# Moving the turns of the row maxima four jobs later in the attention of a transformer block

## The reference, cut to what matters

```python
q = rmsnorm(apply_rope(q, cos, sin), qn_w)
k = rmsnorm(apply_rope(k, cos, sin), kn_w)
k = jnp.repeat(k, rep, axis=2)
v = jnp.repeat(v, rep, axis=2)
scores = jnp.einsum('bthd,bshd->bhts', q, k) / np.sqrt(HD)
scores = jnp.where(causal[None, None], scores, -jnp.inf)
attn = jax.nn.softmax(scores, axis=-1)
out = jnp.einsum('bhts,bshd->bthd', attn, v)
```

## Time and profile before

| | |
|---|---|
| median of 3 runs | 1540.2 us (1532.27 to 1541.4) |
| span of the profiled execution | 1535.8 us |
| busy over the whole span | PE 1313.7, PEld 774.5, DVE 976.1, ACT 692.4, POOL 115.2 us |
| this stage, from its first maximum to its last score | about 1033 to 1325 us of the span |
| stage's steps 0 to 3 | 1046.8 to 1083.4 us |

### The profile page before, as it was taken

One profiled execution on the slowest core, in us unless ns is written; L12 is line 12 of the kernel. 1 busy time (PEld: TensorE's weight loads), 2 busy tenths in 40 slices (PEclk: granted clock), 3 DMA queues, 4 the chain that ended last, 5 costly groups with the idle time before them and its releaser, 6 DMA issues. The chain is left out here.

```text
span 1535.8 us, 21410 instructions
## 1 busy us (share of the span) xinstructions
PE 1313.7 (86%) x7772; PEld 774.5 (50%) x7772; DVE 976.1 (64%) x1750; ACT 692.4 (45%) x1319; POOL 115.2 (7%) x155
## 2 busy tenths in 40 slices
PE   4688999999999999966999996526898888789998
PEld 3344444454545454444888874413343333256886
DVE  4455464545555454146999985756777666257998
ACT  2232334342424252433666665421566556525664
POOL 0000000000000000000000000120211111020000
PEclk9698999999999999987999998855899989868998
DMA  3101111120201020104576640022222210102220
GB/s 103 40 15 34 29 34 34 33 48 15 48 19 43 15 43 15 30 0 96 130 159 146 150 92 1 1 35 90 56 55 57 47 47 20 43 21 78 76 103 28
DMA packets 51476, 81.61 MB, mean 53 GB/s; under 512 B 16749, under 2 KB 34453, under 8 KB 47445
## 3 DMA queue, kind: packets, MB, share of 16 engines
q1 hardware_dynamic: 51004, 79.40, 21.1%
q10 hardware_dynamic: 384, 1.05, 0.6%
HBM read 63.75 MB, written 5.68 MB: 45 GB/s over the span
## 5 line engine op out<-in xcount | busy, mean ns | idle before, releaser
L621 DVE TENSOR_REDUCE mraw<-ps 128x1 f32<-128x512 f32 (+3 forms) x304 | 192.7, 659 | 131.1 <-PE ps L507 74.0
L1329 PE MATMUL ps<-qA 128*128 128x512 f32 x960 | 252.9, 400 | 15.2 <-POOL qA L1439 10.6
L723 ACT ACTIVATE shared<-ps 128x512 f32<-128x512 f32 (+1 forms) x216 | 119.4, 567 | 263.3 <-PE ps L540 261.9
L1046 DVE TENSOR_REDUCE mraw<-ps 128x2 f32<-128x1024 f32 (+3 forms) x160 | 173.7, 1114 | 67.6 <-PE ps L954 46.1
L1329 PEld LDWEIGHTS ps<-qA 128*128 128x128 f32 x960 | 182.1, 192 | 64.2 <-POOL qA L1439 12.3
L1101 ACT ACTIVATE shared<-ps 128x512 f32<-128x512 f32 (+2 forms) x320 | 154.4, 561 | 124.7 <-PE ps L970 124.4
L539 PE MATMUL ps<-qA,kH 128*128 128x512 f32 (+3 forms) x384 | 167.8, 447 | 5.8 <-DMA qB<-mT 5.8
L501 PE MATMUL ps<-kH,qA 128*128 128x512 f32 (+3 forms) x384 | 138.8, 415 | 34.9 <-DVE qA L611 18.8
L1393 ACT CAST qA<-shared 128x512 fp32r<-128x512 f32 x160 | 99.3, 621 | 90.4 <-DVE shared L1531 88.9
L1341 PE MATMUL ps<-qA,kH 128*128 128x512 f32 x480 | 136.3, 393 | 4.1 <-DVE qA L1455 4.1
L540 PE MATMUL ps<-qB,kL 65*128 65x512 f32 (+3 forms) x384 | 132.8, 356 | 0.0
(11 more groups left out here) (247 smaller groups left out, 1747.1 us busy)
## 6 DMA issues: line engine op xcount, KB each, us to landing
shared<-comb SPq DMA_DIRECT2D x92, 256.0 KB, 4.3
qB<-qA SPq DMA_DIRECT2D x16, 512.0 KB, 4.8
rB<-a0rec_dram SPq DMA_DIRECT2D x60, 128.0 KB, 2.9
shared<-comb SPq DMA_DIRECT2D x7, 1024.0 KB, 4.4
rB<-a1rec_dram SPq DMA_DIRECT2D x28, 128.0 KB, 2.6
e0wUp<-in_w SPq DMA_DIRECT2D x48, 64.0 KB, 4.6
qA<-q_split SPq DMA_DIRECT2D x24, 128.0 KB
q_split<-qA SPq DMA_DIRECT2D x4, 512.0 KB
```

Source lines behind the costliest of these rows:

```text
L621: nc.vector.tensor_reduce(out[:, h0:h0 + n_h, qt % 4], src, AX, ALU.max).then_inc(w_free, 1)
L723: nc.scalar.activation(probs(n)[:, hs[0]:hs[-1] + 1, lo:512], src, ACT.Exp, scale=scale)\
L1046: nc.vector.tensor_reduce(out[:, :, js[0]:js[-1] + 1, qt % 4], src, AX, ALU.max).then_inc(x_free, 1)
L1329: ins = nc.tensor.matmul(bank[0:M, :], w[par][:, at:at + M], h[:, cols], start=(r == 0), stop=(r == 2))
```

## The change

The list of jobs is written in another order. The first turn of all stays. Every other turn of half 0 now stands behind the first four maxima of half 1 of its group, and every turn of half 1 behind the first four maxima of the next group. So each of them is four indices later (half 0 of group g: from 22g+6 to 22g+10; half 1: from 22g+21 to 22g+25); the very last turn keeps its index 175. The fold is part of the turn and moves with it. The last step over which the jobs are spread is 84 instead of 85. The list of waits on SP keeps its order; only the count that `rows` waits for follows its turn.

```diff
-    GROUP_JOBS = [("max", 0, j) for j in range(len(MAXES[0]))] + [("turn", 0, 0)] + \
-                 [("max", 1, j) for j in range(len(MAXES[1]))] + [("turn", 1, 0)]
-    NJ = len(GROUP_JOBS)
+    def jobs_of(g):
+
+        some = [("max", g, 0, j) for j in range(len(MAXES[0]))]
+        more = [("max", g, 1, j) for j in range(len(MAXES[1]))]
+        if g == 0:
+            return some + [("turn", 0, 0, 0)] + more
+        return some[:4] + [("turn", g - 1, 1, 0)] + some[4:] + more[:4] + [("turn", g, 0, 0)] + more[4:]
+
+    JOBS = [job for g in range(G) for job in jobs_of(g)] + [("turn", G - 1, 1, 0)]
+    turn_at = {job[1:3]: idx for idx, job in enumerate(JOBS) if job[0] == "turn"}
+    NJ = len(JOBS) // G
...
-        last = NU * (G - 1) + 1
+        last = NU * (G - 1)
...
-                    sp.wait_ge(x_free, NJ * g + (BEFORE if qc == 0 else NJ))
+                    sp.wait_ge(x_free, turn_at[g, qc] + 1)
```

More of the change, by code:

```diff
@@ L923, in max_job @@
                 def max_job(idx):
-                    g, j = divmod(idx, NJ)
-                    kind, qc, n = GROUP_JOBS[j]
+                    kind, g, qc, n = JOBS[idx]
                     pair = pair_banks(idx)
@@ L934, in max_job @@
                         return
-                    if j == 0:
+                    if qc == 0 and n == 0:
                         pe.wait_ge(in_ld[g % 3], landed(g))
```

## The result

Three runs of the changed kernel took 1568.1 us (median; 1566.4 to 1568.3), beside 1540.2 before. The ratio is 1.0201, with a 95% interval of 1.0154 to 1.0248: slower, clear of noise, though the interval doesn't say whether by more or less than 2%. The profiled execution has a span of 1566.6 us, 30.8 more than that of before. The change made the kernel slower, by 28 us in the medians and 31 by the ratio; 32 were forecast.

A forecast was written before the change was run, and what follows sets the result against it. TensorE was taken to bound the stage. Reciprocals +34.2, multiplications +4, folds -3.6 and steps 0 to 3 -2.5 summed to +32 us on 1540.2, forecasting 1572 us, range 1554 to 1592 (about 0.8).

The forecast's parts named there:

- The second way: On SP, rows of half 0 ahead of spread delay the reciprocals' DMAs and so the multiplications; 4 us.
- TensorE's lost lead: Half 0 transposes need folds behind waiting reciprocals: TensorE stops for wait + 0.7 us (groups 2, 3), about the wait (4, 5).
- The chain of 14.2 us: From the end of a half 1 turn's copy, through rows, loads and sums on SP, to the reciprocal: 14.2 us.
- +34.2 for the reciprocals: VectorE's longer waits for sums, with TensorE's lost lead and low clock: 44.4 less the old 10.2 us.
- +4 for the multiplications: Multiplications wait for reciprocals' DMAs behind rows of half 0; bounds 0 to 12.5 us, 4 taken.
- -3.6 for the folds: TensorE's idle time for folds in turns from step 9 on: 10.6 us before, 7.0 after.
- Those stand ahead of both: The four jobs stand ahead of fold and transpose alike, so they do not hide TensorE's wait for a fold.
- Steps 0 to 3: Step 3's fold, 3.01 us beside a memset, starts later: gain about 2.5 us, nothing if it meets following memsets.
- A: Rival: VectorE's waits are absorbed, only half of the new 24.7 us reaches the end; +6, 1546 us; chance 0.10.
- C: Rival: moved turns do nothing, fold waits as before, sums little later, each side within 5 us; 1540; chance 0.05.
- D: Rival: multiplications wait in full (+8.5 more), TensorE's clock stays low longer; 1588 us; chance 0.20.
- B: Rival: faster, SP's loads overlap so sums are not later, only gains left; -6, 1534 us; chance 0.05.

The follow-up runs named there:

- e3: Changed kernel with an iteration's 12 loads on SP moved from ahead of the sums to behind spread; ratio 1.0027, +4 us.
- e11: e2 with the 12 loads on SP moved behind spread; ratio 0.9927, -11 us against the kernel before.
- e2: Of the changed kernel only the turns of half 1 moved, half 0 as before; ratio 1.0119, +18 us.
- e4: Kernel before, old job list, with the 12 loads on SP moved behind spread; ratio 0.9933, -10 us.
- e8: Of the changed kernel only the turns of half 0 moved, with spread ahead of the rows of half 0 on SP; ratio 1.0069, +11 us.
- e5: Changed kernel with SP's order sums, spread, rows of half 0, loads: e3 plus spread first; ratio 0.9951, -8 us.
- e7: Changed kernel with the fold taken out of the turn, right behind its half's last maximum; SP unchanged; ratio 1.0138, +21 us.
- e9: Changed kernel with only spread put ahead of the rows of half 0 on SP; ratio 1.0154, +24 us.
- e6: e5 with the fold taken out of the turn, right behind its half's last maximum; ratio 0.9911, -14 us against the kernel before.
- e10: Kernel before, old job list, with SP's order as in e5 (loads late, spread first); ratio 0.9927, -11 us.

## Why the prediction was right, point by point

**The mechanism.** Late turns of half 1, behind them loads and sums, and VectorE waiting at the reciprocal: shown by e3 and e11, which move only the loads and take 27 us off the changed kernel and 29.5 off e2, while the same edit takes 10 off the old list (e4). The second way, the rows of half 0 ahead of `spread`, is shown by e8 and by e5 against e3. TensorE's lost lead rests on the timelines and on e7.

**The sizes of the waits.**

| group whose turn of half 1 is late | 1 | 2 | 3 | 4 | 5 | 6 | sum |
|---|---|---|---|---|---|---|---|
| forecast | 2.8 | 6.6 | 6.4 | 7.4 | 10.5 | 2.4 | 36.1 |
| measured | 4.56 | 5.93 | 5.83 | 7.18 | 7.43 | 0.44 | 31.4 |

The chain of 14.2 us from the copy's end to the sums held: 14.4, 13.8, 14.1, 13.7 (1229.77 - 1216.09) and 13.7 us (1270.98 - 1257.29) in groups 1 to 5. What was off is when VectorE gets to the reciprocal. In group 5 the turn, the first job of a wide step, ended 1.0 us after the step's start (1256.32), not 1.7, and VectorE was at the reciprocal 7.2 us after that start (1270.98 - 7.43 - 1256.32), where I had counted 1240.5 - 1235.1 = 5.4. I had taken 0.9 us off for the turn that moves behind the reciprocal; the steps didn't get shorter by it. Group 6 errs the same way. In group 1 it is the other way round: from the copy's end (1103.02) to VectorE's arrival (1112.86) 9.8 us passed instead of 11.4, so its wait was longer.

**Their price.** Forecast for steps 4 to 87: +34.2 for the reciprocals, +4 for the multiplications, -3.6 for the folds, together +34.6. Measured +35.7. That this fits so closely is partly luck, as the same stretch by groups shows (the forecast's price of each wait less what the earlier trace rows gave for the old one; the multiplications and the folds are not in it):

| steps | 4 to 15 | 16 to 27 | 28 to 39 | 40 to 51 | 52 to 63 | 64 to 75 | 76 to 87 | sum |
|---|---|---|---|---|---|---|---|---|
| forecast, reciprocals | 0 | 2.6 | 8.5 | 9.1 | 5.1 | 7.4 | 1.5 | 34.2 |
| measured, everything | 3.5 | 5.2 | 4.4 | 8.0 | 5.7 | 1.6 | 7.4 | 35.7 |

The 3.5 us ahead of the first reciprocal are the clock of steps 4 to 15 and in no term. The multiplications were about right in size and wrong in place: e9 takes their waits away and with them 4.8 us of steps 4 to 87, where 4 had been forecast, but 3.5 of these lie in steps 76 to 87. There one multiplication waited 4.07 us behind a turn in step 77, while those of steps 55 and 67, named as signs, waited 0 and 0.76. "I take 4, since slow steps follow every such wait" fitted groups 2 to 5; in group 6 the reciprocal had waited only 0.44 us, and no slow steps covered the multiplication. Without the clock and the multiplications 27.4 us are left (35.7 - 3.5 - 4.8) for reciprocals and folds together, beside 30.6 forecast: the reciprocals came too high, as did their waits, 36.1 against 31.4 us and in group 5 most of all.

**TensorE's lead.** In groups 4 and 5 it stopped for 7.25 and 7.84 us where VectorE had waited 7.18 and 7.43, so one job ahead bought nothing, as forecast; in groups 2 and 3 it stopped for 6.51 and 6.57 us, 0.6 and 0.7 more than VectorE's waits, as forecast too. e7 gives the lead back and takes away the waits for folds: 10 us together.

**The folds.** Apart from the four transposes behind a waiting reciprocal, those from step 9 on waited 7.7 us, forecast 7.0. "Those stand ahead of both" was right: e5's transposes still wait 15.4 us; only with the fold taken out (e6) do they not.

**Steps 0 to 3.** The fold met the next memsets and took 0.99 us instead of 3.01:

```profile
1074.16 1.93 POOL L1122 MEMSET qA<- 1x1024 f32 x2
```
```profile
1075.13 0.99 DVE L1037 COPY mmax<-mraw 128x16 f32<-128x16 f32 x1
```

So 2.0 of the 2.5 us, and steps 0 to 3 were 1.9 us shorter. That this is the work of the moved turn is shown by the other kernels: in all five whose turns of half 0 stand in the old place (before, e2, e4, e10, e11) these steps take 36.5 to 36.7 us, in the nine others 33.9 to 34.9.

**The rivals.** A (1546) and C (1540) needed VectorE's waits to be absorbed or the sums to be late by little, but the waits grew by 20 us and the span by 30.8. D's multiplications waited 6.1 us in all, and 1568 lies far under its 1588. For B, SP's chain had indeed no gap to give, and the rule of the Trainium skill to issue early ("DMA: Bandwidth & Descriptors", "Rules for kernel authors") agrees with e3, e4 and e11: what decided was when four small DMAs were issued.

## What to carry to other kernels

When a job is moved, look at who else stands in line behind it: here a turn with three steps and more to spare was tied, through one SP list, to DMAs that had none. Put small, urgent DMAs ahead of bulk loads that aren't due for a group; that alone was worth 10 us before any turn was moved. And when the profile books an idle time on a producer (L940 waiting for L1037), ask what the producer itself waited for, since removing the named wait (e7) moved most of the idle time to the next instruction. And when a forecast's total fits, check it by stretches: here groups that were off by up to 6 us cancelled.

## What the runs showed of the hardware that I had not expected

The cost of a pause of TensorE is not its length alone: in steps 16 to 87, 19.4 us more idle time came with 12.8 us more busy time for as many matmuls, at a mean granted clock of 0.83 instead of 0.95. The clock also makes differences that no edit explains: steps 4 to 15, ahead of any wait for sums, took 31.8 us at a mean clock of 0.96 in e4 and 35.5 at 0.80 in e10, which have the same list of jobs and differ on SP only behind the first sums. The small copy of the fold ended together with GpSimd's memset in three different places: 3.01 us long before, 0.99 after, and 3.38 in e2 and e4, while the same copy takes 0.17 us elsewhere. The Trainium skill, "SBUF — State Buffer", section "Who interferes with whom", says that a copy in one of VectorE's 2-port modes and GpSimd contend for a shared pair of ports, and that whoever issues first blocks the other fully. The trace agrees with it before and in e2 and e4, in that the copy begins after the memset (1074.54 and 1074.01 before), doesn't slow it and ends with it; which mode the copy ran in no run here shows.
